# Six local layers written out instead of looped, and the first layer norm run between two groups of input loads

## The reference

```python
def _layernorm(x, axis=-1, eps=1e-05):
    m = jnp.mean(x, axis=axis, keepdims=True)
    v = jnp.var(x, axis=axis, keepdims=True)
    return (x - m) / jnp.sqrt(v + eps)

x = x + jnp.tanh(g_xattn[0]) * _L0_xattn_ref(_layernorm(x, axis=-1), ctx_1024, ...)
x = x + jnp.tanh(g_ffn[0]) * _L0_ffn_ref(_layernorm(x, axis=-1), ...)
...

# _L0_ffn_ref: six local layers, one after the other
for i in range(DEPTH):
    x = attn_layer(shift_tokens(x), Wqkv[i], q_scale[i], k_scale[i], Wo[i]) + x
    x = ffn_layer(shift_tokens(x), ln_g[i], ln_b[i], W1[i], b1[i], W2[i], b2[i]) + x
```

## Time and profile before

| what | value |
|---|---|
| time, median of 3 runs | 3145.81 us (3143.45 to 3153.49) |
| the profiled execution's own time | 3153.18 us |
| its span, first to last instruction | 3151.4 us |
| mean granted clock of PE | 0.945 of full speed |
| busy share of the span | PE 86%, DVE 64%, ACT 63%, POOL 50% |
| instructions | 74744 |
| local layers (d = 0 to 5) | from 268.5 to 2284.9 us |

### The profile page before, as it was taken

How to read it: one execution, slowest core, us unless ns; L and a number is a source line. 1 busy time by engine, 2 the same in 40 slices (tenths; PEclk the granted TensorE clock), 3 DMA queues, 4 the chain that set the end, 5 groups by cost and what they waited for, 6 DMA issues and landing times. The chain is left out here.

```text
span 3151.4 us, 74744 instructions
## 1 busy us (share of the span) xinstructions
PE 2724.9 (86%) x27218; PEld 1724.5 (55%) x27218; DVE 2025.1 (64%) x3872; ACT 1985.0 (63%) x5960; POOL 1581.5 (50%) x1845
## 2 busy tenths in 40 slices
PE   4896999799988998899889998899879977996895
PEld 1553766366745775477647664677524433652552
DVE  3664887488847885688658874787445534755673
ACT  3344888488857887588858884888523333555343
POOL 0423887188827884588638881788223102410430
PEclk9798999999999999999999999999979988998797
DMA  2001000100010001000010001000100000000000
GB/s 96 1 2 44 17 19 17 41 17 17 19 39 18 17 17 38 20 17 18 14 44 17 17 19 40 17 17 17 34 7 2 1 1 0 2 2 0 1 2 14
DMA packets 35860, 58.58 MB, mean 19 GB/s; under 512 B 7184, under 2 KB 32656, under 8 KB 33808
## 3 DMA queue, kind: packets, MB, share of 16 engines
q1 hardware_dynamic: 35472, 53.52, 5.4%
HBM read 27.28 MB, written 1.05 MB: 9 GB/s over the span
## 5 line engine op out<-in xcount | busy, mean ns | idle before, releaser
L1037 POOL TENSOR_TENSOR l_qk<-l_ta,l_tb 128x256 f32<-128x256 f32 x768 | 539.5, 739 | 114.9 <-DVE l_tb L1091 114.9
L1053 POOL TENSOR_TENSOR l_qk<-l_qk,l_rn 128x512 f32<-128x512 f32 x384 | 392.8, 1044 | 217.0 <-DVE l_rn L1113 217.0
L660 POOL TENSOR_SCALAR qmr<-q_all,cf 128x256 fp32r<-128x256 f32 x128 | 116.2, 925 | 718.7 <-SPq L461 380.0
L692 DVE TENSOR_REDUCE mrow<-ring 128x2 f32<-128x512 f32 x512 | 324.5, 685 | 190.8 <-PE ring L508 182.1
L958 ACT ACTIVATE l_pr<-st,l_mn 128x128 f32<-128x128 f32 x1152 | 407.6, 383 | 38.6 <-DVE l_mn L1079 38.6
L1044 POOL TENSOR_TENSOR l_pr<-l_pr,l_rs 128x512 f32<-128x512 f32 x384 | 393.8, 1052 | 42.5 <-DVE l_rs L1103 42.5
L645 ACT ACTIVATE pt<-st 128x512 f32<-128x512 f32 x384 | 200.2, 600 | 286.6 <-PE st L543 286.6
L1095 DVE TENSOR_REDUCE l_n<-l_sq 128x8 f32<-128x512 f32 x384 | 262.9, 686 | 177.4 <-ACT l_sq L967 175.1
L958 ACT ACTIVATION_READ_ACCUMULATOR l_pr<-st,l_mn 128x1 f32 x1152 | 255.4, 222 | 0.0
L821 PE MATMUL ring<-l_wa,l_xs 128*128 128x512 f32 x384 | 201.2, 648 | 42.3 <-DVE l_xs L1074 28.5
L533 PE MATMUL st<-qm,k_all 32*128 32x512 f32 x1024 | 219.8, 664 | 0.0
(11 more groups left out here) (237 smaller groups left out, 6370.3 us busy)
## 6 DMA issues: line engine op xcount, KB each, us to landing
l_vm<-l_v SPq DMA_DIRECT2D x192, 96.0 KB, 2.0
l_wa<-in_wa SPq DMA_DIRECT2D x7, 2048.0 KB, 9.2
l_vm<-l_v SPq DMA_DIRECT2D x192, 32.0 KB, 1.9
l_wf<-in_wf SPq DMA_DIRECT2D x6, 580.5 KB, 4.5
w<-in_w SPq DMA_DIRECT2D x1, 2752.0 KB, 15.8
cf<-in_cf SPq DMA_DIRECT2D x1, 1253.0 KB, 7.7
x<-in_xT SPq DMA_DIRECT2D x1, 1024.0 KB, 5.2
ctxT<-in_ctxT SPq DMA_DIRECT2D x1, 1024.0 KB, 9.7
```

The lines of the kernel that those rows point to most:

```text
L692: dve.tensor_reduce(mrow[b % 2][:, t, j, 2 * p:2 * p + 2], bank_of(f"R{r}").rearrange("p (h k) -> p h k", h=2), AX.X, ALU.max).then_inc(ri ...
L1037: ins = pool.tensor_tensor(halves[0][:, :, x], halves[1][:, :, x], halves[2][:, :, 1 - x], ALU.add)
L1053: pool.tensor_tensor(part, part, t.rn[:, :, 4 * x:4 * x + 4].unsqueeze(3).broadcast_to([P, 2, 4, LHD]), ALU.mult).then_inc(qk_normed, 1)
```

## The change

It does three things. The loop over d becomes a Python loop, so that the six layers stand one after the other in each engine's list, and every wait compares with a constant. The loads are split in two blocks: the first issues all transfers, with x, the first 260 columns of cf and the gates ahead, and waits for these alone; the second waits for the rest and makes padcol and padrow. The first layer norm stands between the two. For this, the tables that it reads are moved to the front of cf.

```diff
-    f["ident"] = eye
     f["mean"] = np.full((P, P), 1.0 / P)
     f["center"] = eye - 1.0 / P
+    for n, v in (("eps5", 1e-5), ("eps6", 1e-6), ("eps3", 1e-3), ("lnoff", 10 * np.log(2.0))):
+        f[n] = np.full((P, 1), v)
+    f["ident"] = eye
...
-def load_everything(g, tmp):
+def start_loads(g, pad_r, pad_c):
...
+    n = F_AT["ident"]
     with nc.Block() as block:
         @block.sync
         def _(sp):
-            for dst, src in loads:
-                sp.dma_start(dst, src).then_inc(loaded, 16)
-            sp.wait_ge(loaded, 16 * len(loads))
+            sp.dma_start(g.x[:, :], a["xT"]).then_inc(first_loaded, 16)
+            sp.dma_start(g.cf[:, 0:n], a["cf"][:, 0:n]).then_inc(first_loaded, 16)
+            sp.dma_start(g.gates[:, :], a["gates"].broadcast_to([P, 8])).then_inc(gates_loaded, 16)
...
+            sp.wait_ge(first_loaded, 32)
 
         @block.scalar
         def _(act):
-            act.wait_ge(loaded, 16 * len(loads))
+            act.wait_ge(gates_loaded, 16)
             act.activation(g.gates[:, :], g.gates[:, :], ACT.Tanh).then_inc(prepared, 1)
+
+
+def finish_loads(g, pad_r, pad_c):
+    nc = g.nc
+    loaded = g.sem("inputs_loaded")
+    with nc.Block() as block:
+        @block.sync
+        def _(sp):
+            sp.wait_ge(loaded, 16 * 8)
 
         @block.vector
         def _(dve):
-            dve.wait_ge(loaded, 16 * len(loads))
...
+            dve.wait_ge(loaded, 16 * 8)
+            dve.tensor_scalar(g.padcol[:, :], pad_c, 0.0, MASKED, ALU.is_equal, ALU.mult)
+            dve.tensor_scalar(g.padrow[:, :], pad_r, 0.0, g.f("padval", 1), ALU.is_equal, ALU.mult)
...
-    with nc.Fori(0, DEPTH) as d:
+    for d in range(DEPTH):
         local_attention(g, d, t)
         local_ffn(g, d, FfnMemory(t))
...
-        phase(load_everything, g)
+        def load(tmp):
+            pad_r, pad_c = tmp("pad_r", [P, TOK], I32)[:, :], tmp("pad_c", [P, 2 * NB], I32)[:, :]
+            start_loads(g, pad_r, pad_c)
+            norm(g.x, g.y, "eps5")
+            finish_loads(g, pad_r, pad_c)
+
+        phase(load)
         for l in range(4):
             if 2 * l >= stop:
                 break
-            norm(g.x, g.y, "eps5")
+            if l:
+                norm(g.x, g.y, "eps5")
```

More of the change, by code:

```diff
@@ L98, in constants @@
     e = np.arange(EXPERTS)
-    for n, v in (("eps5", 1e-5), ("eps6", 1e-6), ("eps3", 1e-3), ("lnoff", 10 * np.log(2.0))):
-        f[n] = np.full((P, 1), v)
     f["earlier"] = np.broadcast_to((e[None, :] < e[:, None]).reshape(1, -1) * 1.0, (P, EXPERTS * EXPERTS))
@@ L195, in cols @@
     return bass.ds(c * width, width)
-def load_everything(g, tmp):
+def start_loads(g, pad_r, pad_c):
     nc, a = g.nc, g.a
[L201 to L207, removed]
+    first_loaded, gates_loaded, loaded = g.sem("first_loaded"), g.sem("gates_loaded"), g.sem("inputs_loaded")
+    prepared = g.sem("gates_prepared")
+    n = F_AT["ident"]
     with nc.Block() as block:
@@ L210, in _ @@
         def _(sp):
-            for dst, src in loads:
-                sp.dma_start(dst, src).then_inc(loaded, 16)
-            sp.wait_ge(loaded, 16 * len(loads))
+            sp.dma_start(g.x[:, :], a["xT"]).then_inc(first_loaded, 16)
+            sp.dma_start(g.cf[:, 0:n], a["cf"][:, 0:n]).then_inc(first_loaded, 16)
+            sp.dma_start(g.gates[:, :], a["gates"].broadcast_to([P, 8])).then_inc(gates_loaded, 16)
+            sp.dma_start(g.ctxT[:, :], a["ctxT"]).then_inc(loaded, 16)
+            sp.dma_start(pad_r, a["pad_r"].broadcast_to([P, TOK])).then_inc(loaded, 16)
+            sp.dma_start(pad_c, a["pad_c"]).then_inc(loaded, 16)
+            sp.dma_start(g.w[:, :], a["w"]).then_inc(loaded, 16)
+            sp.dma_start(g.cf[:, n:], a["cf"][:, n:]).then_inc(loaded, 16)
+            sp.dma_start(g.cb[:, :], a["cb"]).then_inc(loaded, 16)
+            sp.dma_start(g.v[:, :], a["v"]).then_inc(loaded, 16)
+            sp.dma_start(g.rbias[:, :], a["rbias"].broadcast_to([P, 2 * EXPERTS])).then_inc(loaded, 16)
+            sp.wait_ge(first_loaded, 32)
         @block.scalar
         def _(act):
-            act.wait_ge(loaded, 16 * len(loads))
+            act.wait_ge(gates_loaded, 16)
             act.activation(g.gates[:, :], g.gates[:, :], ACT.Tanh).then_inc(prepared, 1)
+def finish_loads(g, pad_r, pad_c):
[5 more added lines that the diff above has]
+            sp.wait_ge(loaded, 16 * 8)
         @block.vector
         def _(dve):
-            dve.wait_ge(loaded, 16 * len(loads))
-            dve.tensor_scalar(g.padcol[:, :], pad_c[:, :], 0.0, MASKED, ALU.is_equal, ALU.mult)
-            dve.tensor_scalar(g.padrow[:, :], pad_r[:, :], 0.0, g.f("padval", 1), ALU.is_equal, ALU.mult)
+            dve.wait_ge(loaded, 16 * 8)
+            dve.tensor_scalar(g.padcol[:, :], pad_c, 0.0, MASKED, ALU.is_equal, ALU.mult)
+            dve.tensor_scalar(g.padrow[:, :], pad_r, 0.0, g.f("padval", 1), ALU.is_equal, ALU.mult)
 def layernorm(g, use, src, out, eps, tmp, scale=None, shift=None):
```

## The result

| what | before | after |
|---|---|---|
| median of 5 runs each, us | 3146.89 (3143.45 to 3153.49) | 3126.73 (3124.91 to 3131.3) |
| the profiled execution's own time | 3153.18 | 3126.73 |
| span | 3151.4 | 3124.9 |
| granted clock of PE, mean | 0.945 | 0.946 |
| instructions | 74744 | 70010 |

The ratio after to before is 0.9934, with a 95% interval of 0.9923 to 0.9945: the change makes the kernel 20 us faster. The forecast was 3110, with a range of 3091 to 3129. The time lies in the range, at its slow end, and the gain is 0.56 of the 35.7 us forecast. The profiled execution of before was 6.3 above its median, that of after was the median itself, so the two traces differ by 26.5, not by 20.

A forecast was written before the change was run, and what follows sets the result against it. PE, busy 86%, is the busiest engine, but the change targets its idle stretches. Gains of 12.4 + 18.3 + 3.5 + 1.5 = 35.7 us from the median 3145.81 give 3110 (chance 0.79), range 3091 to 3129.

The forecast's parts named there:

- The jump back: Passages between local layers: five DVE idle times, 20.0 us in all, go and 1.75 stays in their place; 18.3 us faster.
- PE's clock at the passages: Each layer's first matmuls would run at the higher clock level after a shorter idle time; 3.5 us faster, 0.7 per passage.
- PE is thinly used until the pipeline is full, and a drop there costs too: Start of each layer: a clock drop behind the first matmuls also costs, so 0.7 per passage was taken instead of 1.5.
- The start: Program start: first norm runs beside the remaining transfers, first projection near 24.1 instead of 36.5; 12.4 us faster.
- in one more transfer; I give 0.3: Loads at the start: the same bytes in one more transfer would cost 0.3 us, with bounds 0 and 1.
- the 22 that the prediction names as a sign of being wrong: Program start: a first norm that ends behind 22 us would show the forecast wrong.
- The register instructions: All engines' lists, every step of every layer: their removal would save 1.5 us, with bounds 0 and 8.
- the fused instruction: Attention, ahead of the minima in one step of four: its removal saves 0.03 us each, over 8 steps and 6 layers.
- A wait on a constant is not faster: Waits in all engines: a constant gives 0.03 us behind its releaser, a register value 0.04, so no gain was counted.
- a head start that fails at the start of the program: Rival: late gates or a norm held up beside the transfers lose the 12.4 us, time 3122; chance 0.06.
- The lock: Rival, attention steps: the DVE and POOL order at their shared ports turns, 50 us more gain, time 3060; chance 0.10.
- The lower clock: Rival: PE's lower clock holds for 37 us at the start of each of five layers, time 3187; chance 0.03.

The follow-up runs named there:

- e5: The kernel before with only the tables of cf in their new order; 3147.02 us, ratio 0.9996 to before.
- e1: The kernel before with the new split loads and the norm between them, the loop over d kept; 3145.32 us, ratio 0.9993 to before.
- e11: e1 plus a block behind the local layers in which DVE fills a 1536-column scratch tile; 3155.25 us, ratio 0.9987 to before.
- e7: The changed kernel with the small transfers pad_c, v, rbias and cb issued ahead of ctxT, pad_r, the rest of cf and w; 3125.50 us, ratio 0.9927 to before.
- e4: The changed kernel with the late wait for ACT's copies stated ahead of the two others before PE's matmul; 3127.74 us, ratio 0.9946 to before.
- e3: The changed kernel with a loop of three passes over two layers each, so two jumps back remain; 3129.36 us, ratio 0.9939 to before.
- e6: The changed kernel plus a block behind the local layers in which DVE fills a 1536-column scratch tile; 3122.97 us, ratio 0.9919 to before.

## Why the prediction was right or wrong

The forecast was 3110, the time 3126.73. The gain is there and its largest term, the jump, is right; the terms of the start and of the register instructions failed, and the rest of the program, taken as unchanged, was not.

**The jump back, forecast 18.3.** Right: 17.5. Five idle times of 20.0 in all became 1.6.

**PE's clock at the passages, forecast 3.5.** The mechanism was right. Between the two traces it is 6.5 − 0.2 = 6.3, near the upper bound of 7.4. The first matmuls run at the higher level, and DVE's wait of 2.17 is 1.36. The drop behind them, for which I cut the term in half, comes in every layer of after, with a third step of 10.3 in three of the five and a second of 9.8 in the other two. But three of before's five had it too (10.1, 11.2, 11.1 for the third), so it cost only 0.2 more. This depends on the execution that is compared: of the traces with the loop, e5 and e1 have the drop in two layers of the five, before and e11 in three, and the same sum (first floor and three steps of five layers) is 3.1, 3.4, 6.3 and 7.1 above that of after. So 3.5 lies within what the runs show. "PE is thinly used until the pipeline is full, and a drop there costs too" was true of both kernels.

**The start, forecast 12.4.** It was 10.95 at the first projection. The step that failed is "in one more transfer; I give 0.3": padcol started 1.5 later than forecast, since two of the small transfers at the tail of SP's list took 1.31 and 0.74 to issue; e7 puts them first and has 24.19. The tanh of the gates ended late too, and the norm began at 8.76 instead of near 7.6; it then took 13.6 instead of 12.4, since its first eight matmuls took 6.47 where they took 5.22 (no run takes apart whether by the transfers or by PE's clock). It ended at 22.39, behind the 22 that the prediction names as a sign of being wrong. It cost nothing only because padcol was late as well: at the forecast 22.2 the norm would have been the one to wait for. The larger error is what the term was taken for. It was added to the sum as if a lead at 25 us were a lead at the end. e1 shows some 2 us of it left, at most 6.

**The register instructions, forecast 1.5.** Wrong, and this is the step that failed within the layers: taking the instructions out made the steps 2.9 slower in sum (4.2 − 1.3). The 0.03 that was put down to the fused instruction is there: the step of 8.56 that before has once in four is 8.53, 1.3 in all. Not foreseen was that the waits which rode on register instructions need an instruction of their own, and that the order of three waits then decides which one PE holds: +0.10 in one step of four, 0.10 × 7 × 6 = 4.2 (e4 shows the cause). Between the two traces the attention blocks gained 1.9, which is 6.3 of the clock less 4.4; the 1.5 that are still missing lie in layer 0 behind its last floor (23.9 us to the end of the block, where before has 22.4), and the granted clock there is 0.81 in the last 17.6 us of the block, against 0.90 in the last 16.6 of before. "A wait on a constant is not faster" looked at a wait that stands alone; where several stand ahead of one instruction it can be slower.

**The rest of the program, forecast 0.** It was +4.1 between the two traces (+6.1 against e5), with PE busy 4.7 more for the same 6322 matmuls and the other engines busy alike to 0.3: it is PE's clock.

**The sum.** 35.7, less 1.3 (start), 0.8 (jump), 5.9 (register instructions) and 4.1 (rest), and 2.8 more for the clock, is 26.4, the difference of the two traces. The remaining 6.3 is the profiled execution of before, which lay above its median, where that of after did not. That the time lies in the range is in part luck: the range's slow end was set for a head start that fails at the start of the program (3122) and for the clock at the passages, and not for a head start that is there and is lost later, which is what e1 shows.

**The rivals.** The lock kept its order in every layer, as the 0.79 supposed. The head start didn't fail. The lower clock held for 3.5 or 6.8 us at a time in the five later layers, not for 37. Straight code starves nothing: PE's attention blocks are as long as before.

## What to carry to other kernels

Each jump back of this loop held the passage up by 3.5 us, and where every iteration starts with a handover through all engines, writing a few iterations out is worth that pause times their number and not more. When several waits on constants stand ahead of one matmul, state first the one that ends last: here the matmul held the wait stated first, and an extra instruction the others. The small instruction of VectorE that showed 1.06 us for 16 columns was held by GpSimd: a wait that orders the two was worth more than everything that this change removed. And a gain read at one place of a program is a gain at the end only if the clock lets it through, so check the untouched stages of both traces before you explain the total.

## What the runs showed of the hardware

- PE's compare-and-branch of 3.5 us is a price of the jump alone: DVE idles 4.4 at each of e3's two jumps and 0.3 at the passages between.
- The same 4030 matmuls of untouched code took from 516.4 to 529.4 us in fourteen programs. DVE, ACT and POOL were busy alike to 0.4 us in the four windows shown, so these 13 us are PE's granted clock: more than the 11 us of the head start.
- Within one kernel the runs lie up to 20 us apart (e1, 3139.28 to 3159.20), so differences of 3 us between versions, that of e6 among them, can't be told by the time. The steps in the trace can.
- Where three waits on constants stand ahead of a matmul, the matmul holds the one stated first and an instruction of PE's list (L894, 51 ns) the two others. A matmul behind the late wait in that instruction starts 0.14 after its releaser instead of 0.05.
